# Three moves in VectorE's order of work, at the seam between attention and experts

## The reference, cut to what matters

```python
x = x + xattn(layernorm(x), ctx, ctx, Wq, Wk, Wv, Wo, bo, masks)   # 8 batches x 256 tokens x 256, 16 heads
def ffn(x):                                   # 2048 tokens, 8 experts, 2 chosen, hidden size 1024
    gate = softmax(flat_x @ w_gate.T)
    topk_scores, topk_idx = top_k(gate, 2)
    cw = (one_hot(topk_idx, 8) * topk_scores[..., None]).sum(axis=1)
    h = gelu(einsum('td,edh->teh', flat_x, W1) + b1)
    y = einsum('teh,ehd->ted', h, W2) + b2
    return einsum('ted,te->td', y, cw)
x = x + ffn(layernorm(x))
```

## Time and profile before

| what | value |
|---|---|
| median of 3 runs | 506.69 us (506.08 to 507.53) |
| the profiled execution | 508.38 us |
| its span, first to last instruction | 507.0 us |
| TensorE matmuls busy | 443.7 us, 88% |
| VectorE busy | 363.7 us, 72% |
| ScalarE busy | 326.5 us, 64% |
| GpSimd busy | 175.0 us, 35% |
| mean granted TensorE clock | 0.955 |

### The profile page before, as it was taken

How to read it: one execution, slowest core, us unless ns; L and a number is a source line. 1 busy time by engine, 2 the same in 40 slices (tenths; PEclk the granted TensorE clock), 3 DMA queues, 4 the chain that set the end, 5 groups by cost and what they waited for, 6 DMA issues and landing times.

```text
span 507.0 us, 10200 instructions
## 1 busy us (share of the span) xinstructions
PE 443.7 (88%) x3586; PEld 374.6 (74%) x3586; DVE 363.7 (72%) x803; ACT 326.5 (64%) x523; POOL 175.0 (35%) x220
## 2 busy tenths in 40 slices
PE   5798979998968986969989797999999999999892
PEld 3355656676756653558989797999889898898882
DVE  4556776777766874567879984987777879689651
ACT  2123775676645644749869674988686967869650
POOL 5146241372508437030554422242221422222213
PEclk9898999999989997898989899999999999999978
DMA  7693624324123114660576599698787796887702
GB/s 234 197 252 122 219 105 136 118 87 136 70 82 127 67 55 148 254 263 19 203 231 218 170 279 326 219 270 244 232 239 277 212 307 195 264 293 214 222 12 34
DMA packets 44624, 93.19 MB, mean 184 GB/s; under 512 B 6990, under 2 KB 30350, under 8 KB 38684
## 3 DMA queue, kind: packets, MB, share of 16 engines
q1 hardware_dynamic: 35340, 81.56, 47.7%
q0 software_dynamic: 7152, 9.46, 9.4%
q10 hardware_dynamic: 2080, 1.49, 1.0%
HBM read 63.10 MB, written 14.32 MB: 153 GB/s over the span
## 4 chain that ended last, share of the span: by engine, by line
PE 46%; DVE 15%; DMA 13%; ACT 10%; issue 10%; SPq 4%; POOL 1%; another core or an unknown queue 0%; ACTq 0%; DVEq 0%; POOLq 0%
DMA w_in<-in_W 8%; PE bank L1393 8%; PE S L1357 7%; PE bank L1460 6%; DVE nmax L951 5%; PE S L1492 5%; PE bank L1452 3%; ACT hf L1169 3%; PE bank L1527 3%; PE bank L1443 3%; PE S L1515 2%; PE bank L1435 2%; ACT W2p L1141 2%; ACT Q L1129 2%; DMA lists<-zero 2%
## 5 line engine op out<-in xcount | busy, mean ns | idle before, releaser
L582 POOL DMA_INDIRECT out<-y,slot x39 | 69.9, 1791 | 176.2 <-DVE y L859 102.0
L951 DVE TENSOR_REDUCE nmax<-S 128x4 f32<-128x1024 f32 x64 | 78.3, 1224 | 49.2 <-PE S L1492 49.1
L1357 PE MATMUL S<-xgT,Q 128*128 128x256 f32 x512 | 97.3, 289 | 1.6 <-DVE xgT L825 1.4
L1265 ACT ACTIVATE prob<-S 128x1024 f32<-128x1024 f32 x64 | 65.8, 1028 | 33.4 <-PE S L1515 32.3
L1357 PEld LDWEIGHTS S<-xgT,Q 128*128 128x128 f32 x512 | 80.0, 192 | 2.7 <-issue 2.7
L1393 PE MATMUL bank<-W2p,hp 128*128 128x256 f32 x528 | 71.3, 294 | 5.5 <-DVE y L855 5.5
L802 DVE TENSOR_TENSOR K<-w_in,Q 128x1024 fp32r<-128x1024 f32 x46 | 55.9, 1223 | 24.6 <-ACT Q L1129 23.5
L1169 ACT ACTIVATE hf<-S,b1c 128x256 f32<-128x256 f32 x128 | 53.1, 467 | 30.8 <-PE S L1357 26.9
L1357 PE MATMUL S<-xgT,K 128*128 128x256 f32 x256 | 72.7, 284 | 0.0
L1393 PEld LDWEIGHTS bank<-W2p,hp 128*128 128x128 f32 x528 | 67.7, 200 | 5.8 <-issue 5.8
L841 DVE TENSOR_TENSOR hp<-hf,hp 128x512 fp32r<-128x512 f32 x64 | 44.1, 689 | 19.4 <-ACT hp L1189 19.3
(11 more groups left out here) (211 smaller groups left out, 818.7 us busy)
## 6 DMA issues: line engine op xcount, KB each, us to landing
w_in<-in_W SPq DMA_DIRECT2D x46, 1024.0 KB
K<-flat_k SPq DMA_DIRECT2D x24, 256.0 KB, 2.4
Q<-flat_q SPq DMA_DIRECT2D x24, 256.0 KB
xg<-lists SPq DMA_DIRECT2D x16, 265.0 KB
b_in<-in_b SPq DMA_DIRECT2D x23, 128.0 KB
lists<-zero SPq DMA_DIRECT2D x9, 265.0 KB
cin<-in_ctxT SPq DMA_DIRECT2D x8, 256.0 KB, 3.9
xin<-in_x SPq DMA_DIRECT2D x8, 256.0 KB, 4.1
```

Of the source, the lines that this page charges most:

```text
L582: st_y[i % 4].after(pool.indirect_dma_start(out=out, out_offset=bass.IndirectOffsetOnAxis(ap=slot[i % 4][:, t:t + 1], axis=0), in_=y[i % 2 ...
L951: max_done.after(dve.tensor_reduce(nmax[n % 4][:, :, :, m].rearrange("p t r -> p r t"), S1[:].rearrange("p r (t k) -> p r t k", t=TT), AX. ...
L1265: exp_done.after(act.activation(prob[s % 4][:].rearrange("p r t l -> p (r t l)"), S2[:].rearrange("p r l -> p (r l)"), ACT.Exp, scale=SCALE))
L1357: ins = pe.matmul(h_bank[pair][:, u, 0:n], W1p[k][a][:, kc, m * P:(m + 1) * P], xgT[k][c][:, kc, 0:n], start=(j == 0), stop=(j == len(term ...
```

## The change

VectorE does the same 780 rows of instructions in another order; no other engine's order changes.

1. `LATE_BACK[7]["divide"]` goes from 75 to 74, and TensorE's `div` stays at 75. In step 74 the division stands ahead of the list work and of unit (0, 0).
2. `scaled_sum` is split into `summed` (waits for `y_done`, adds) and `scaled`. In pair 3 of tiles 1 to 7 `summed(i - 1)` stands at the head of the unit, ahead of `hidden_low` and `w2_low`; `scaled(i - 1)` stays at its end.
3. `rows_low` is split into `rows_known` (register, b1c, slot, scale) and `rows_low` (the low part). Only for tile 0 are they apart: `rows_known(0)` stands in step 71, `rows_low(0)` in step 72.

```diff
+    SUMS_FIRST = EARLY
...
-        7: dict(div=75, divide=75, ao=76, aT=77, o=78, add=78, store=79, ln2=78, norm2=79, y=81, yT=82)}
+        7: dict(div=75, divide=74, ao=76, aT=77, o=78, add=78, store=79, ln2=78, norm2=79, y=81, yT=82)}
...
         def dve_unit(u):
             i, pair = divmod(u, 4)
+            if pair == 3 and 0 < i <= SUMS_FIRST:
+                summed(i - 1)
             if HT[i] > 1:
                 hidden_low(i, pair)
...
             if pair == 1 and i + 1 < NTILE:
+                rows_known(i + 1)
                 rows_low(i + 1)
             if pair == 3 and i:
-                scaled_sum(i - 1)
+                if i - 1 >= SUMS_FIRST:
+                    summed(i - 1)
+                scaled(i - 1)
...
+                if s == PE_STEP - 1:
+                    rows_known(0)
                 if s == PE_STEP:
                     rows_low(0)
```

More of the change, by code:

```diff
@@ L809, in w2_low, with rows_known @@
                                           ALU.subtract))
-        def rows_low(i):
-            k, c, n = i % 2, column[i], HT[i] * P
+        def rows_known(i):
+            k, c = i % 2, column[i]
             dve.wait_ge(table_done.sem, stage_of(i))
@@ L823, in rows_low @@
                                              .rearrange("p t o -> p (t o)")))
+        def rows_low(i):
+            k, n = i % 2, HT[i] * P
             dve.wait_ge(xg_hi.sem, i + 1)
@@ L842, in hidden_low, with summed @@
                                          hp[i % 2][0][:, c, 0:n].bitcast(F32), ALU.subtract))
-        def scaled_sum(i):
+        def summed(i):
             k = i % 2
@@ L854, in scaled_sum, with scaled @@
             for t in range(HT[i]):
-                now = y_sum.after(dve.tensor_tensor(y[k][:, t], y_bank[:, t], b2_in[i % 3][:], ALU.add))
+                y_sum.after(dve.tensor_tensor(y[k][:, t], y_bank[:, t], b2_in[i % 3][:], ALU.add))
+        def scaled(i):
+            k = i % 2
             dve.wait_ge(scale_done.sem, i + 1)
             for t in range(HT[i]):
-                dve.wait_ge(y_sum.sem, now - HT[i] + 1 + t)
+                dve.wait_ge(y_sum.sem, halves_to(i) + 1 + t)
                 y_out.after(dve.tensor_scalar(y[k][:, t], y[k][:, t], scale[i % 4][:, t:t + 1], None, ALU.mult))
@@ L880, in dve_experts @@
                 dve_unit(u)
-            scaled_sum(NTILE - 1)
+            summed(NTILE - 1)
+            scaled(NTILE - 1)
         def dve_attention():
```

## The result

| | changed | before |
|---|---|---|
| median, runs | 508.92 us (12) | 506.65 us (12) |
| lowest to highest | 507.53 to 514.0 us | 502.85 to 514.69 us |
| the profiled execution | 508.61 us | 508.38 us |
| its span | 507.1 us | 507.0 us |

The ratio is 1.0069, with a 95% interval of 1.0043 to 1.0095: slower by about 3.5 us, where the prediction had 505.8 and a range up to 507.3. Every ratio here leaves out slow runs, those over 1.5% above the fastest run of the same kernel (here two of the kernel before, at 510.5 and 514.69, and none of the changed one). The medians lie 2.3 us apart. The two profiles end within 0.1 us of each other, so they can't be compared by their ends. They are compared by stages.

The account below looks back on a forecast made before the run. Bound: one chain of waits from batch 7's division through VectorE's unit (3, 3) and SyncE's zero rows to tile 7's rows. -0.78 - 1.88 + 1.4 + 0.4 = -0.86 us, from median 506.69 to 505.8 us; range 504.0 to 507.3.

Parts of the forecast that it names:

- The slots: First tile's register load hides behind a low part, removing VectorE's idle time before the bias copy: 0.78 us gained.
- The start of the division and the two pauses: Batch 7's division starts once its operand is there; TensorE's 4.84 us pause becomes two, about 1.1 and 3.6 us.
- The room for it: With the division ahead of VectorE's list work, product (1, 0) starts 2.66 us sooner, 0.78 of it already counted.
- The clock takes part of it back: TensorE's clock falls behind the split pause ahead of product (1, 0): 1.4 us lost, between 0 and 1.83.
- the 1.26 us: Net gain from product (1, 0) on: 2.66 us sooner less 1.4 us lost to the clock.
- The sums, SyncE: In unit (3, 3) tile 5's W2 load and bias wait, so SyncE's later issues, zeros included, come 0.4 us later.
- The sums, all that follows: Sums ahead cost 0.4 us in all, bounds 0 to 1.8; VectorE's waits in units (4, 3) to (7, 3) priced 0.
- D: As rival, not stage time: sums make VectorE wait for TensorE, delaying tile 9's W2 load; slower, up to 508.5; 10%.
- B: Rival: TensorE's clock stays up behind the split pause, nothing is lost; 2.0 us less, 504.7 us; 20%.
- C: Rival: gain lost on the way, register load not hidden or a later pause meeting a slow spell; 506.3 to 507.1; 25%.

Follow-up runs that it names:

- The turnings: 24 identity transposes, results overwritten, put into TensorE's pause ahead of product (1, 0) of the changed kernel: ratio 0.9956 against the kernel before, 1.0044 without them.
- the pairs with turnings: Kernels with and without sums ahead, against the kernel before: 0.9956 and 0.9895 with turnings ahead of product (1, 0), 0.9880 and 0.9826 with turnings at tile 7 too.
- the second comparison: The changed kernel, unaltered, run again beside the kernel before on another chip: 502.55 us, ratio 1.0044.
- the early zeros: SyncE's eight zero transfers issued inside tile 5's loads instead of tile 6's: ratio 0.9967 with slots alone, 0.9982 with all edits, against the kernel before.
- The second group of turnings: 24 more identity transposes ahead of tile 7's rows, added to division, slots and the first turnings, sums not ahead: 496.50 us, ratio 0.9826 against the kernel before.

## Why the prediction was wrong

- **The slots: right.** The idle time ahead of the copy is gone, 0.78 us. Alone they give 0.9990, which can't be told from nothing.
- **The start of the division and the two pauses: right as a mechanism.** 0.97 and 3.47 us against "about 1.1 and 3.6", in all profiles but the first, where a delay of 1.87 us came in between.
- **The room for it: mis-sized.** "2.66 us sooner" took VectorE's idle time of 3.17 us from one profile. It is 1.81 in the others. Product (1, 0) starts 15.42 us behind the first low part with division and slots, 16.59 with slots alone: 1.17 us sooner where 1.88 were forecast, and that only because product (0, 3) is no longer slow.
- **"The clock takes part of it back": mis-sized, by how much is not settled.** I priced the loss at 1.4 us with a bound of 1.83, the loss of the one spell before. But the spell before began inside TensorE's pause, where a low clock costs nothing, and covered product (0, 3), which with the division ahead is over long before product (1, 0) can start. With the pause cut in two it begins near the start of product (1, 0), costs nearly its full length, and can last: 0.63 over 9.2 us in the first profile. A is 1.4 us longer by the mean (45.2 against 43.8 for the three undelayed profiles), and 1.0 longer (44.85) if the profile with the late division is left out on this side too, where I had it shorter by 0.5; three of the six profiles are no longer than without the division. In time, division and slots without the sums are at 0.9986 (0.9946 to 1.0026), which has room for the 1.26 us that I forecast for them. The turnings, which take the spell away and change nothing else, give 0.0088 back; a part of that the kernel before loses as well.
- **The sums, SyncE: right.** The first zero row's issue is 0.34 to 0.71 us later in six of the seven profiles and 1.47 in the first one, against the 0.4 of the sum, with 0.52 between W2 and bias.
- **The sums, all that follows: the step that failed.** I let 0.4 us pass through to the end and no more, and read the pause of 2.8 us up to 312.57 as one that leaves the clock up. It did so in that profile, but the clock fell behind three of the eight pauses without sums ahead (2.88 to 3.64 us) and behind all nine with them (3.14 to 5.53 us). D is 1.2 us longer or more in all nine. In time the sums cost 0.0034 alone and 0.005 to 0.007 in the pairs with turnings, 1.7 to 3.7 us, against my bounds of 0 to 1.8. 0.4 to 0.7 and the 1.5 of D are seen in profiles; the rest is not placed, and that the sums make the clock fall there, and not chance, is argued from nine profiles against eight.
- **The rivals.** D forecast the sign, with a price up to 508.5, but not the reason. Its wait is there (1.54 us in unit (7, 3)) and its W2 load is late, and neither ends a pause: cover held. B's premise, the clock stays up, is what the turnings make true by force: division, slots and turnings are at 0.9895 and 0.9882. Whether the division pays then, or the turnings alone would do it, no run shows. C had the form of the failure, a pause that falls so that it meets a slow spell that it escaped before, with its price too low and at a place I had not looked at.

The sum of 0.9 us gained, then, became a loss of 3.5 us (2.2 in the second comparison). By the times it is the sums that carry it: without them, division and slots are at 0.9986, not to be told from before. The profiles add low clock on product (1, 0) in the changed kernel, of which the times can't say how much is new. My account of both is one mechanism, a pause of TensorE moved or lengthened so that low clock falls on work that others wait for; it is shown for the pause ahead of product (1, 0), and argued for that ahead of tile 7. The range, too, was a little wider than its terms: C's upper end is 507.1, not 507.3.

**A version that beats both** is division and slots ahead, sums where they were, turnings ahead of product (1, 0): 0.9895 and 0.9882 with 6 runs each, and 0.9887 (0.9847 to 0.9927) with 12 runs and the early zeros, some 5.7 us under the kernel before. The second group of turnings (0.9826 by three runs) can't be told from none.

## What to carry to other kernels

Before you shorten or move a wait of TensorE's, write down what it does in the 10 us behind the wait and whether others wait for that: here a spell of low clock that began inside a pause cost little, and one on the products behind it did not. Price an idle time from more than one profile, by a point of the program near it and not by the span's start. Where a pause can't be filled with work, a few microseconds of matmuls into a bank that is overwritten anyway can be worth more than the reordering; try them in the kernel as it was, too, which was not done here.

## What the runs showed that I had not expected

- 2.78 us of useless turnings in one pause are worth 0.88% (1.0044 to 0.9956), and they raise no wait of their own: 0.83 us of the pause is left behind them.
- Two profiles of one kernel have the same pause to 0.01 us (2.87 and 2.88) and different clocks behind it (1.00 and 0.66).
- D takes one of two values to within 0.02 us in most profiles, 24.1 or 25.6. Part of what looks like scatter of the times is such spells, 1.5 us each in D and in A.
- Eight zero transfers in a time when SyncE issues nothing are not free: tile 6's rows took 12.53 us to land instead of 5.59 (slots with early zeros, and slots alone).
- With 12 runs of a kernel the 95% interval is 0.3 to 0.5% to either side. The times alone hardly tell these edits apart; stages counted from a near point tell more, but need several profiles each.
